# Stage A of a gated cross-attention block: norm 4's steps moved forward on three engines, and turn2 reads after two passes

## The reference, cut to what matters

```python
z = self_attn(x, Wq1, Wk1, Wv1);          x = layer_norm(x + z, ln1_g, ln1_b)
z = cross_attn(x, context, Wq2, Wk2, Wv2); x = layer_norm(x + z, ln2_g, ln2_b)
z = relu(x @ fc1_w + fc1_b) @ fc2_w + fc2_b
out = layer_norm(x + z, ln3_g, ln3_b)
x = x_in + tanh(g_xattn[0]) * out
h = _layernorm(x)                     # norm 4 below (norms count from 0)
gate = silu(bitlinear(h, w_gate)); up = bitlinear(h, w_up)
x = x + tanh(g_ffn[0]) * bitlinear(gate * up, w_down)
# bitlinear: the activation is rounded to integers, scaled by 127 / max|.| of its row; weights to -1, 0, 1
```

## Time and profile of the kernel before

| what | value |
|---|---|
| median of 3 executions | 2424.04 us |
| profiled execution, its own time | 2430.15 us |
| its span, first to last instruction | 2428.3 us |
| mean granted TensorE clock | 0.905 |
| busy: TensorE, VectorE, ScalarE, GpSimd | 2046.4, 1585.8, 1320.4, 534.5 us |
| last part of stage A: first residual2, last copy (L513) | 404.94, 641.60 us |
| granted clock from 404.94 to 646.40 us | 0.57 |
| granted clock in stage B, 646.40 to 1849.00 us | 0.98 |

### The profile page before, as it was taken

One profiled execution on the slowest core, in us unless ns is written; L12 is line 12 of the kernel. 1 busy time (PEld: TensorE's weight loads), 2 busy tenths in 40 slices (PEclk: granted clock), 3 DMA queues, 4 the chain that ended last, 5 costly groups with the idle time before them and its releaser, 6 DMA issues. The chain is left out here.

```text
span 2428.3 us, 45160 instructions
## 1 busy us (share of the span) xinstructions
PE 2046.4 (84%) x17914; PEld 1362.0 (56%) x17914; DVE 1585.8 (65%) x3854; ACT 1320.4 (54%) x2169; POOL 534.5 (22%) x476
## 2 busy tenths in 40 slices
PE   4779997466499999999999999999996888878997
PEld 3546665243255655555565565556564565556776
DVE  4834453677478778788788778778862566653443
ACT  3645553465326666666666666656673545543333
POOL 1410001443122122122122122212212233211111
PEclk8789997565569999999999999999997889969999
DMA  5036662000122232233233223223212100000000
GB/s 158 1 92 179 195 180 65 4 14 21 51 94 94 80 115 104 73 110 114 67 108 115 76 102 113 82 93 114 101 56 93 35 29 24 1 1 4 8 8 11
DMA packets 89103, 181.18 MB, mean 75 GB/s; under 512 B 5906, under 2 KB 63162, under 8 KB 88510
## 3 DMA queue, kind: packets, MB, share of 16 engines
q1 hardware_dynamic: 88894, 178.30, 22.4%
HBM read 95.24 MB, written 11.65 MB: 44 GB/s over the span
## 5 line engine op out<-in xcount | busy, mean ns | idle before, releaser
L1407 DVE TENSOR_REDUCE b_part_max<-psum 128x1 f32<-128x482 f32 (+3 forms) x1248 | 737.4, 650 | 188.3 <-PE psum L1284 174.2
L1197 ACT ACTIVATE b_PT<-psum 128x800 f32<-128x800 f32 x768 | 616.3, 836 | 386.3 <-PE psum L1303 380.1
L1284 PE MATMUL psum<-b_KH,b_QBD 64*128 64x482 f32 (+1 forms) x1152 | 422.5, 445 | 45.8 <-DVE b_part_max L1407 43.4
L1303 PE MATMUL psum<-b_QS,b_KS 64*128 64x200 f32 x3072 | 438.4, 288 | 0.5 <-ACT b_PT L1197 0.3
L1303 PEld LDWEIGHTS psum<-b_QS,b_KS 64*128 64x128 f32 x3072 | 339.4, 186 | 16.2 <-issue 11.8
L1319 PE MATMUL psum<-b_PT,b_V 128*32 128x200 f32 x6144 | 341.3, 339 | 0.6 <-ACT b_PT L1197 0.6
L1284 PEld LDWEIGHTS psum<-b_KH,b_QBD 64*128 64x128 f32 x1152 | 197.4, 189 | 198.1 <-DVE b_part_max L1407 118.3
L1120 POOL TENSOR_TENSOR b_KL<-b_KF,b_KH 128x1444 fp32r<-128x1444 f32 x32 | 106.9, 3341 | 693.0 <-PE psum L1303 670.0
L1319 PEld LDWEIGHTS psum<-b_PT,b_V 128*32 128x32 f32 x6144 | 160.0, 109 | 149.2 <-ACT b_PT L1197 82.3
L2095 DVE SCALAR_TENSOR_TENSOR c_U<-psum,c_gt,c_U 100x128 f32<-100x128 f32 x256 | 72.1, 344 | 130.3 <-PE psum L1916 130.0
L384 POOL TENSOR_TENSOR a_rs<-a_ve,a_half 100x4 f32<-100x4 f32 x48 | 49.1, 1022 | 426.2 <-DVE a_ve L757 426.2
(11 more groups left out here) (274 smaller groups left out, 3235.0 us busy)
## 6 DMA issues: line engine op xcount, KB each, us to landing
b_KS<-b_KH SPq DMA_DIRECT2D x64, 722.0 KB
a_CT<-in_ctxt SPq DMA_DIRECT2D x32, 722.0 KB, 4.2
b_CT<-in_ctxt SPq DMA_DIRECT2D x32, 722.0 KB, 4.3
b_KS<-b_KL SPq DMA_DIRECT2D x32, 722.0 KB
a_CN<-in_ctxn SPq DMA_DIRECT2D x32, 704.0 KB
att_scratch<-b_AO SPq DMA_DIRECT2D x32, 200.0 KB, 1.9
c_AIN<-att_scratch SPq DMA_DIRECT2D x8, 800.0 KB
b_MB<-in_mask SPq DMA_DIRECT2D x32, 180.5 KB, 4.4
```

The source lines that it names most:

```text
L1197: nc.scalar.activation(PT[:, kt % 2, 2 * a:2 * a + 2, :], psum[:, 2 * a:2 * a + 2, 0:TG], ACT.Exp).then_inc(sem["pt_ready"], 1)
L1284: m = mm(bank(b, D, size), QBD[rows, j % 2, tile * D:(tile + 1) * D], KH[rows, j % 2, at_:at_ + size], start=True, stop=True)
L1303: m = mm(bank(p, D, 2 * T, (s % 2) * 2 * T), KS[rows, j % 2, s, kt * D:(kt + 1) * D], QS[rows, j % 2, s * 2 * T:(s + 1) * 2 * T], start=Tr ...
L1407: v.tensor_reduce(part_max[0:rows, q, c:c + 1], bank(b, rows, CHUNKS[c][1]), AX.X, ALU.max)\
```

## The change

All edits are in the last part of stage A.

1. GpSimd, gain2: the pass that makes norm 2's output with its own shift comes second rather than third and writes into U; the pass for YB comes third, with a signal of its own, `yb_ready`.
2. TensorE: turn2 reads U and not Y2. VectorE: residual3 also waits for `yb_ready`.
3. GpSimd: rstd(4) stands ahead of gain2.
4. ScalarE: normalise(4) stands ahead of gate(2) and turned2.
5. VectorE: outcome stands ahead of inner(0).

```diff
                 pl.tensor_tensor(Y2[:, p, :, :], Y2[:, p, :, :], row("ln2g"), ALU.mult).then_inc(sem["scaled2"], 1)
                 pool.wait_ge(sem["scaled2"], u + 1)
-                pl.tensor_tensor(YB[:, p, :, :], Y2[:, p, :, :], bias2[:, :].unsqueeze(1).to_broadcast([T, GROUP, D]), ALU.add)
-                pl.tensor_tensor(Y2[:, p, :, :], Y2[:, p, :, :], row("ln2b"), ALU.add).then_inc(sem["y2_ready"], 1)
+                pl.tensor_tensor(U[:, p, :, :], Y2[:, p, :, :], row("ln2b"), ALU.add).then_inc(sem["y2_ready"], 1)
+                pl.tensor_tensor(YB[:, p, :, :], Y2[:, p, :, :], bias2[:, :].unsqueeze(1).to_broadcast([T, GROUP, D]), ALU.add)\
+                    .then_inc(sem["yb_ready"], 1)
...
-            ticks(((gain3, 1), (rstd(2), 0), (gain2, 0), (rstd(4), 1), (rstd(5), 3), (rstd(3), 0)), UNITS + 3)
+            ticks(((gain3, 1), (rstd(2), 0), (rstd(4), 1), (gain2, 0), (rstd(5), 3), (rstd(3), 0)), UNITS + 3)
...
                    (normalise(2, lambda u: U[:, u % 2], lambda u: Y2[:, u % 2]), 0),
-                   (inner_turned(3), 3), (gate(2), 2), (turned2, 0),
-                   (normalise(4, lambda u: X[:, u % 4], lambda u: H[:, u % 3]), 1),
-                   (rectify, 0), (gate(3), 2), (turned3, 1), (gate(0), 1),
+                   (inner_turned(3), 3), (normalise(4, lambda u: X[:, u % 4], lambda u: H[:, u % 3]), 1),
+                   (gate(2), 2), (turned2, 0), (rectify, 0), (gate(3), 2), (turned3, 1), (gate(0), 1),
                    (normalise(5, lambda u: X[:, u % 4], lambda u: U5[:, u % 2]), 3), (gate(1), 1)), UNITS + 4)
...
-                turn(0, Y2[:, u % 2], turned[2])
+                turn(0, U[:, u % 2], turned[2])
...
                 dve.wait_ge(sem["f2_psum"], u + 1)
+                dve.wait_ge(sem["yb_ready"], u + 1)
                 link(v.tensor_tensor(U3[:, p, :, :], tok_bank(1), YB[:, p, :, :], ALU.add))
...
-            ticks(((residual2, 0), (inner(0), 2), (outcome, 1), (inner(1), 2), (leave, 3),
+            ticks(((residual2, 0), (outcome, 1), (inner(0), 2), (inner(1), 2), (leave, 3),
                    (quantise, 1), (inner(2), 2), (residual3, 0), (inner(3), 2), (scale_inner, 2)), UNITS + 3)
```

More of the change, by code:

```diff
@@ L109 @@
 max2_ready pT_psum pT_ready quant_ready r2_psum rT2_ready rT_ready r_psum row_ready s1_psum s2_psum s2m_psum scaled1
-scaled2 scaled3 sm1_ready v1_psum v1_ready y1_ready y2_ready y3_ready z1_psum z2T_psum z2T_ready z2_psum
+scaled2 scaled3 sm1_ready v1_psum v1_ready y1_ready y2_ready y3_ready yb_ready z1_psum z2T_psum z2T_ready z2_psum
 """.split()
```

## The result

The changed kernel took 2407.41 us (median of 7 executions, 2401.97 to 2412.85) against 2424.04 us for the kernel before in the same session (7 executions), 16.6 us less. The ratio on record is 0.992 with a 95% interval of 0.9898 to 0.9943, which is 14 to 25 us; it is not the quotient of the two medians, which is 0.993. So the median lies inside the range and the ratio just outside it. Over all sessions together the changed kernel's 13 executions average 2407.9 us and the 71 of the kernel before 2425.9, 18.1 less. The direction and the ring came out as forecast; the size was too small.

What follows compares the result with a forecast made beforehand. A ring of waits, no single engine, bounds stage A's second half. Savings of 1.2, 1.1 and 2.4 us (ticks 0 to 2), 6.9 (ticks 3 to 6) and 1.6 (tick 7) make 13.2: 2410.8 us, range 2405.5 to 2418.0.

Steps and rivals of the forecast that it cites:

- the ring: Second half of stage A: circle of waits from residual2 through norm 2, turn2, norm 4, quantise, residual3 to values2.
- Ticks 0 to 2: First ticks of stage A's second half, cut at residual2's starts: savings of 1.2, 1.1 and 2.4 us.
- Ticks 3 to 6: Stage A's second half: four ticks of 22.5 us each, 90.0 instead of 96.9, saving 6.9 us.
- Tick 7 and the draining ticks: End of stage A: tick 7, last with a residual3, saves 1.6 us; draining ticks wait for the down chain, 0.
- Rival B: Stage A's second half: TensorE's clock rises, outer product takes 1.12 us, ticks 21.7; time 2406.8 us, chance 0.16.
- Rival C: Stage A's second half: the clock sinks, ticks at 23.5 us, 7.3 us saved; time 2416.7 us, chance 0.12.
- Rival A: Gain2's passes: only the pass counts, eight times 1.2 is 9.8 us saved; time 2414.2 us, chance 0.13.
- The second effect: ScalarE: norm 5 starts only 1.22 us earlier, so gate(1) stands 0.4 us behind it, delaying norm 3 and norm 2.
- The shared ports: GpSimd and VectorE: root of rstd(2) stretched to 1.49 us, hidden; root of rstd(5) may hold quantise's scaling 0.4 us.
- E: VectorE's outcome waits for y3, gain3's output: if over 3 us late, slower than before, 2435 us; chance 0.06.
- The other signs: Signs of being right: residual3 idle about 0.9 us for the outer product; stage B's first instruction 13 us earlier.

Runs made afterwards that it cites:

- x2_order: The kernel before with only the three orders changed (rstd(4), normalise(4), outcome), gain2's passes left as they were: 2420.04 us, ratio 0.9971.
- x4_rstd: The changed kernel with rstd(4) put back behind gain2, normalise(4) still ahead of turned2: 2441.33 us, ratio 1.0058.
- x5_bfill: The kernel before with 8 idle transposes added in TensorE's wait ahead of turn2: 2423.68 us, ratio 0.9992.
- x6_afill: The changed kernel with 3 idle transposes added in TensorE's wait ahead of turn2: 2407.22 us, ratio 0.9911.
- x7_norm5: The changed kernel with normalise(5) moved ahead of gate(0) on ScalarE: 2409.26 us, ratio 0.9928.
- y3_noact: The changed kernel with ScalarE's order put back, normalise(4) behind turned2: 2420.24 us, ratio 0.9985.
- x3_noout: The changed kernel with outcome put back behind inner(0) on VectorE: 2412.11 us, ratio 0.9938.
- y1_awarm: The changed kernel with idle transposes in six kinds of TensorE's waits: 2401.03 us, ratio 0.9905.

## Why the prediction was right or wrong, point by point

- **The ring and its cut: right.** Quantise follows leave, residual3 waits for the outer product, turn2 starts after two passes, rstd(4) is done before gain2 wants GpSimd. From tick 3 on the 2.99 us ahead of quantise are gone and turn2's 2.00 are 0.78. x2_order and x4_rstd show that the places of the steps matter as the ring says.
- **Ticks 0 to 2: nearly right.** 1.2, 1.1 and 2.4 us were forecast; 1.2, 1.5 and 3.0 came.
- **Ticks 3 to 6: the step that failed.** I put all four at 22.5, priced on tick 6 of before, where the outer product took 2.03 us, and so at the low clock from norm 2 to norm 3. For that clock the sum was right: 17.04 less 1.6 is 15.4, and the changed kernel's slow tick 5 took 15.41; the 7.11 from norm 3 on came as 7.12 to 7.44. But three of the four ticks had the fast clock there and took 13.7 to 13.8, with ticks of 20.3 to 20.9 us; together the four took 85.0, not 90.0. Before had such ticks too, 3 and 4 (clock 0.64 and 0.72 in the earlier trace rows, outer product 1.12), but in the old order they were only 0.2 to 0.45 us shorter in this stretch, so their length did not show the price.
- **Tick 7 and the draining ticks: the same step.** Tick 7 went with tick 6, at 1.6. It was a fast one, 13.74 from norm 2 to norm 3 where before took 17.04. In this pair of traces the end of the part gained 2.9 us: with 5.7 in ticks 0 to 2 and 11.9 in ticks 3 to 6 that makes the 20.5.
- **Rival B: the right one, mis-sized and given too little chance.** I took only the 0.9 us of the outer product from a fast tick and then said that VectorE soon limits, 21.7 us. From the outer product's start to gate(0) TensorE and ScalarE alternate: 4.41 us before (558.02 to 562.43), 4.42 in the slow tick 5 now, 2.73 in the fast tick 4 (498.85 to 501.58). That is 1.7 less, and 22.5 - 1.7 = 20.8 is what the fast ticks take. VectorE's own wait at residual3 was still there, 0.25 us, so VectorE did not limit. B's time, 2406.8, lies 0.6 us from the median, and that is in part luck: its fast tick was 0.8 to 1.4 us too long, and it had none at the low clock. Its argument for the clock, the shorter idle stretch before turn2, is not borne out: filling that stretch changed nothing (x5_bfill, x6_afill). The range's lower end hung on B's size, and five of the changed kernel's thirteen executions lie below it.
- **Rival C: its tick was right for the low clock.** It put a tick at 23.5; x6_afill's ticks wholly at 0.50 go from norm 2 to norm 2 in 23.42 and 23.46.
- **Rival A: wrong in its size.** The passes alone bring 3 us, not 9.8; the root behind the third pass took the wait's place. In the kernel before, I had read that normalise(4) "stands in order behind turned2" as the only reason. It was one of two, met within 0.2 us of each other.
- **The second effect, norm 5 ahead of gate(1): only for slow ticks at best.** The 0.4 us forecast are 0.30 at the low clock (15.41 less the 15.11 of x7_norm5) and 0 at the high one, and x7_norm5 gained nothing in time.
- **The shared ports: seen and hidden.** The root of rstd(2) took 1.49 us in ticks 1, 2 and 6 of the changed kernel and 1.02 in ticks 3 to 5 and 7, where gain3 is late and the root starts ahead of outcome. I see no norm 2 that moved by it. The 0.4 us for which the root of rstd(5) might hold quantise's scaling did not come: the scaling (L841) started 1.12 to 1.13 us after quantise's first instruction in ticks 3 to 7, and 1.14 in tick 6 of before, as the root ended about when the scaling began. But in ticks 1 and 2, where quantise falls beside gain2's third pass, the scaling took 1.60 and 1.55 us and not 0.87; residual3 waited for the outer product there anyway.
- **E, the coupling through y3: there, and small.** Outcome waits 1.16 us for y3 in ticks 3, 4, 5 and 7. It was priced from 3 us on; at 1.16 the root is still 0.8 us early. I had named an idle of over 1 us there as a sign of being wrong; it showed, and cost nothing.
- **The other signs.** Residual3 was to idle about 0.9 us for the outer product; by the forecast's own figures, 16.3 less 12.0 + 3.69, it should have read 0.6 to 0.7. It was 1.19 in tick 5, at the low clock, and 0.25 to 0.28 in ticks 3, 4, 6 and 7. Stage B's first matmul started 23.5 us earlier in this pair, not 13.

What is shown: in the stretch that it shortens, the change is worth 1.63 us per tick at the low clock and 2.87 at the higher, because the clock is worth 0.45 us in the old order and 1.69 in the new. At a like mean clock of the run that is 10 to 12 us (three executions against ten), and with idle work in both kernels 20. What is not shown is why a given tick or execution gets the fast clock: two traces of the changed kernel agree to 0.03 us, y3_noact with nearly the same order had none in ticks 4 to 6, and x6_afill, with more work on TensorE, had ticks 3 and 4 at 0.50.

## What to carry to other kernels

When a queue stands behind one wait, look for the second condition that is met just before it; cutting one alone brings next to nothing, and moving a consumer ahead without its producer (x4_rstd) costs more than both bring together (32 to 34 us against 17 to 18). Before taking one tick as the measure of all, read the granted clock of each, and price the new ring at both levels: once a reorder has taken the other engine off the ring, TensorE's steps on it count in full, and one of them took 2.03 us at one level and 1.12 at the other. Cut a tick at more than one step before comparing it with others; residual2's start alone was off by up to 1.5 us. A single pair of traces can differ by several microseconds in stages that the change doesn't touch, so take totals from medians.

## What was not expected of the hardware

TensorE's clock brought 2 us per tick of 23 with one and the same program (x3_noout, 0.50 against 0.75), though TensorE was busy for only 13 to 16 us of such a tick. The whole kernel's time went with the mean clock by 10 us per 0.01 over thirteen executions. The Trainium skill, page TensorE: Matmul & The Clock Gate, section "HAM oscillation — how this bites in real kernels", tells of such a clock falling in each iteration of a kernel that waits for DMA in between. Here the waits are for other engines. If they act alike, idle work should help: y1_awarm agrees (6 us by the medians), while x5_bfill and x6_afill (0 us) show that filling one of several waits does not.
